# A batch loop of 16 equal steps: one key and one value tile each, maxima one step behind, context split by quarters

## The reference

```python
# 1. cross attention, 16 heads of 32
qh = layernorm(x) @ wq + bq;  kh = ctx @ wk + bk;  vh = ctx @ wv + bv     # keys: 2048 per batch
x  = x + softmax(qh kh^T / sqrt(32)) vh @ wo + bo
# 2. causal linear attention with relu features, then an MLP 512 -> 2048 -> 512 with GELU
# 3. gated feed-forward 512 -> 1408 -> 512 with blockwise FP4 rounding of activations and weights
```

## Time and profile before

| | |
|---|---|
| median of 3 runs | 3425.43 us (3423.25 to 3429.36) |
| profiled execution | 3425.2 us, span 3423.4 us |
| granted TensorE clock, mean | 0.998 of full |
| PE busy | 3384.3 us (99%) |
| PE weight loads busy | 2628.8 us (77%) |
| DVE busy | 2221.6 us (65%) |
| POOL busy | 2081.4 us (61%) |
| ACT busy | 1200.4 us (35%) |

### The profile page before, as it was taken

One profiled execution on the slowest core, in us unless ns is written; L12 is line 12 of the kernel. 1 busy time (PEld: TensorE's weight loads), 2 busy tenths in 40 slices (PEclk: granted clock), 3 DMA queues, 4 the chain that ended last, 5 costly groups with the idle time before them and its releaser, 6 DMA issues.

```text
span 3423.4 us, 77272 instructions
## 1 busy us (share of the span) xinstructions
PE 3384.3 (99%) x31304; PEld 2628.8 (77%) x31304; DVE 2221.6 (65%) x3425; ACT 1200.4 (35%) x1655; POOL 2081.4 (61%) x1210
## 2 busy tenths in 40 slices
PE   8999999999999999999999999999999999999999
PEld 6777777777777777777777777777777788878887
DVE  6556556555655655655565565566776688789997
ACT  2244343443434434344344343444223322321111
POOL 3277877878777887778877878762545400023332
PEclk9999999999999999999999999999999999999999
DMA  4111110111101100101011010122222333410000
GB/s 152 50 44 38 38 38 29 47 38 38 38 30 47 50 29 35 50 27 51 29 44 42 26 51 29 48 75 76 72 87 83 128 102 101 130 65 19 25 18 19
DMA packets 83368, 182.96 MB, mean 53 GB/s; under 512 B 7184, under 2 KB 43152, under 8 KB 73872
## 3 DMA queue, kind: packets, MB, share of 16 engines
q1 hardware_dynamic: 83088, 178.63, 15.1%
HBM read 140.59 MB, written 38.01 MB: 52 GB/s over the span
## 4 chain that ended last, share of the span: by engine, by line
PE 92%; DVE 4%; issue 2%; ACT 1%; POOL 1%; DVEq 0%; ACTq 0%; POOLq 0%
PE a_bank L100 67%; PE a_bank L1408 8%; PE a_bank L1453 7%; PE a_bank L1417 6%; DVE x_probsT L1263 1%; PE a_bank L712 1%; PE a_bank L2421 1%; ACT x_probsT L1152 0%; PE a_bank L723 0%; PE a_bank L1472 0%; PE a_bank L1441 0%; PE a_bank L777 0%; PE a_bank L781 0%; DVE s_rden L653 0%; PE a_bank L1426 0%
## 5 line engine op out<-in xcount | busy, mean ns | idle before, releaser
L1251 DVE TENSOR_REDUCE x_maxima<-a_bank 128x1 f32<-128x512 f32 x960 | 608.5, 683 | 741.0 <-PE a_bank L1408 741.0
L949 POOL TENSOR_TENSOR x_pairs<-x_probsT 128x1024 f32<-128x1024 f32 x240 | 571.7, 2382 | 298.2 <-ACT x_probsT L1152 292.9
L100 PE MATMUL a_bank<-x_wv,x_ctx 128*128 128x512 f32 x3072 | 746.0, 396 | 1.1 <-ACT q_out L224 1.1
L100 PE MATMUL a_bank<-x_ctx,x_wk 128*128 128x512 f32 x3072 | 743.3, 396 | 0.0
L1152 ACT ACTIVATE x_probsT<-x_probsT 128x1024 f32<-128x1024 f32 x480 | 507.8, 1058 | 642.1 <-DVE x_probsT L1263 642.1
L100 PEld LDWEIGHTS a_bank<-x_wv,x_ctx 128*128 128x128 f32 x3072 | 563.7, 188 | 167.2 <-DVE x_maxima L1251 27.3
L100 PEld LDWEIGHTS a_bank<-x_ctx,x_wk 128*128 128x128 f32 x3072 | 564.7, 188 | 136.7 <-issue 11.9
L1263 DVE TENSOR_TENSOR x_probsT<-a_bank,x_shift_all 128x1024 f32<-128x1024 f32 x480 | 578.7, 1216 | 138.2 <-ACT x_shift_all L1169 120.1
L1417 PEld LDWEIGHTS a_bank<-x_q,x_k 32*128 32x128 f32 x7680 | 240.8, 186 | 115.5 <-issue 63.0
L1147 ACT ACTIVATE x_v<-a_bank 128x512 f32<-128x512 f32 x256 | 153.1, 598 | 420.6 <-PE a_bank L100 420.6
L1077 POOL TENSOR_TENSOR x_ctx<-x_ctx_raw,x_ctx 128x2048 fp32r<-128x2048 f32 x64 | 293.1, 4579 | 5.0
(11 more groups left out here) (207 smaller groups left out, 3992.8 us busy)
## 6 DMA issues: line engine op xcount, KB each, us to landing
x_ctx_raw<-in_ctx SPq DMA_DIRECT2D x64, 1024.0 KB, 4.8
m_ff_src<-in_w_ff SPq DMA_DIRECT2D x44, 192.0 KB, 2.5
wq_ff<-m_ff_dst SPq DMA_DIRECT2D x44, 192.0 KB, 1.8
attT<-x_out_halves SPq DMA_DIRECT2D x16, 512.0 KB, 2.8
s_attT<-attT SPq DMA_DIRECT2D x16, 512.0 KB, 4.0
m_w_raw<-in_w SPq DMA_DIRECT2D x32, 256.0 KB, 2.9
f_w_in<-wq_ff SPq DMA_DIRECT2D x22, 256.0 KB, 3.5
q_x<-in_x SPq DMA_DIRECT2D x16, 256.0 KB, 4.3
```

Source lines behind the costliest of these rows:

```text
L100: mm = pe.matmul(out, lhs[a], rhs[b], start=first and n == 0, stop=last and n == 2)
L949: eng.tensor_tensor(pairs[:], probs(i, s)[:, :, 0:2], probs(i, s)[:, :, 2:4], ALU.add).then_inc(paired, 1)
L1251: dve.tensor_reduce(maxima[:, c, g * HG + j:g * HG + j + 1], banks[:, j], AX.X, ALU.max).then_inc(maxed, 1)
```

## The change

- The batch loop's body is `back(i)` (steps 8 to 15) and then `front(i + 1, i)` (steps 0 to 7 of the next batch), for 14 turns. `front(0)` stands ahead of it, `back(14)` behind it.
- Every step s does `top(s - 1)`, `score(s)`, in even steps two `weigh`, then one key item (`key_bank`: bank 5 in even steps, 4 in odd ones) and one value item (`value_bank`: bank 4 in step 0, bank 0 in all others). The value item of step s is tile s - 4 modulo 16: tiles 12 to 15 of a batch are made in its own steps 0 to 3. `top(15)` and the last two `weigh`, into bank 1, stand behind step 15.
- `score(0)` waits for the last `gather` of the batch before. Step 1 waits for the value item of step 0 to be copied out; then come `denominators` of the batch before, into bank 3, and `top(0)`.
- Two spreads stand between the key and the value item of step 0, one in step 1, one in step 2.
- The context is loaded and split in tiles of 128 rows (`load_tile`, `split_tile`): 256 KB, and two GpSimd operations on 128x512 elements in each step. A tile's split waits for the value item of the same step, whose buffer it overwrites. The key item of steps 0, 4, 8 and 12 waits for all the tiles before it.
- GpSimd's four operations that end a batch are spread over the steps 3 to 6 of the next. The division is done in two halves, in steps 1 and 2, in place. The last gathers write the sums to `x_sums_out`, so that `x_acc` is not read by GpSimd. Each result goes out in two transfers.
- In the first batch the tiles 12 and 13 leave the code ahead of the loop; after the loop four value tiles are made and not two, and the denominators of batch 14 come behind them.

```diff
-            def macro(i):                                    # tensor
...
+            def keys(i, s):
+                c, t = divmod(s, DC)
+                if t == 0:
+                    pe.wait_ge(ctx_made, START + tiles_made(i, s))
+                pe.wait_ge(maxed, START + HG * (NS - 1) + i * (HG * NS) + (HG * s + key_bank(s) - HG + 1))
+                item(i + 1, "k", c, t, key_bank(s), (lambda: turn(i)) if s == 0 else None)
+
+            def values(i, s):
+                if s:
+                    pe.wait_ge(shifted, START + i * (2 * NS) + (2 * s + 1))
+                item(i, "v", *value_tile(s), value_bank(s))
+
+            def step(i, s, past=None):
+                if s == 0:
+                    pe.wait_ge(gathered, START + i * TWINS)
+                    pe.wait_ge(shifted, START + i * (2 * NS))
+                    pe.wait_ge(v_ready, START + values_done(i, -1))
+                    score(i, 0)
+                else:
+                    if s == 1:
+                        pe.wait_ge(v_ready, START + values_done(i, 0))
+                        pe.wait_ge(shift_kept, START + shift_at(i, HG + 2))
+                    if s in (2, 3):
+                        pe.wait_ge(shift_kept, START + shift_at(i, HG + s + 1))
+                    if past is not None and s == 1:
+                        pe.wait_ge(shifted, START + i * (2 * NS) + 2)
+                        denominators(past, 3)
+                    pe.wait_ge(gathered, START + i * TWINS + (s - 1) // 2)
+                    top(i, s - 1)
+                    if past is not None and s == 1:
+                        pe.wait_ge(den_out, START + (past + 1))
+                    pe.wait_ge(shifted, START + i * (2 * NS) + 2 * s)
+                    pe.wait_ge(v_ready, START + values_done(i, s - 1))
                     score(i, s)
+                if s and s % 2 == 0:
+                    await_maxed(i + 1, s - 1, 1)
+                    weigh(i, s - 2)
+                    weigh(i, s - 1)
+                keys(i, s)
+                if s < 3:
+                    for g in ((0, 1), (2,), (3,))[s]:
+                        spread(i, g)
+                values(i, s)
...
+                top(i, NS - 1)                                # back(i), behind step 15
                 pe.wait_ge(shifted, START + i * (2 * NS) + 2 * NS)
+                weigh(i, NS - 2, b=1)
+                weigh(i, NS - 1, b=1)
...
+            def split_tile(i, s):                             # gpsimd
+                hi, lo = (a[:, (s // TPC + 1) % 2, :, cols(s % TPC, P)] for a in ctx_t)
+                raw_t = tile_raw[s % 2]
+                pool.wait_ge(ctx_loaded[s % 2], START + (WHOLE * 16 * (1 - s % 2)) + i * (8 * NS) + 16 * (s // 2 + 1))
+                pool.wait_ge(v_done, START + values_done(i, s))
+                pool.tensor_tensor(hi, raw_t[:], one[:].to_broadcast([P, DC, P]), ALU.mult).then_inc(ctx_made, 1)
+                pool.wait_ge(ctx_made, START + tiles_made(i, s) + 1)
+                pool.tensor_tensor(lo, raw_t[:], hi.bitcast(F32), ALU.subtract).then_inc(ctx_made, 1)
...
+            def step(i, s, past=None, ahead=True):
+                if ahead or s < NS - TPC:
+                    split_tile(i, s)
+                add_up(pool, i, s)
+                if past is not None and 3 <= s < 7:
+                    (normalise, add_bias, out_hi, out_lo)[s - 3](past)
...
+            def first_step(i, past):                          # scalar
                 place_rows(i)
                 copy_spread(i, 0)
+                keys(i, 0)
+                copy_spread(i, 1)
+                exp(i, 0, 0)
+                values(i, 0)
+                if past is not None:
+                    copy_den(past)
+                exp(i, 0, 1)
...
+            def step(i, s, past=None):                        # vector
+                if s:
+                    maximum_by_head(i + 1, s - 1, tops, (0, 1))
+                add_shift(i, s, 0)
+                if s:
+                    maximum_by_head(i + 1, s - 1, tops, (2, 3))
+                add_shift(i, s, 1)
+                if s and s % 2 == 0:
+                    gather(i, s // 2 - 1)
+                if past is not None and s in (1, 2):
+                    invert(past, s - 1)
...
+                maximum_by_head(i + 1, NS - 1, tops, (0, 1, 2))   # back(i), behind step 15
                 gather(i, TWINS - 1)
+                maximum_by_head(i + 1, NS - 1, tops, (3,))
                 negate(i + 1)
...
+            for v in range(TPC):                              # tensor, behind the loop
+                await_maxed(LAST, NS - 1, (2, HG)[v > 0])
+                if v >= 2:
+                    await_item(LAST, "v", NKC - 1, v - 2)
+                item(LAST, "v", NKC - 1, v, (5, 7)[v % 2], (lambda: turn(LAST)) if v == 0 else None)
+            await_item(LAST, "v", NKC - 1, TPC - 2)
+            denominators(LAST - 1, 5)
```

More of the change, by code:

```diff
@@ L858, in attention_phase, with key_bank, value_bank, value_tile @@
     LAST = B - 1
[L859 to L873, removed]
+    ALONE = 8
+    WHOLE = NKC + 1
+    SET_UP = 4
+    KEYS_PER = 1
+    def key_bank(s):
+        return 4 + (s + 1) % 2
+    def value_bank(s):
+        return 0 if s else 4
+    def value_tile(s):
+        return divmod((s - DC) % NS, TPC)
     with ExitStack() as stack:
@@ L1091, in add_bias @@
                 pool.wait_ge(out_made, START + i * 3 + 2)
[L1092 to L1111, removed]
+                pool.tensor_tensor(lo[:], sums_out[:], hi[:].bitcast(F32), ALU.subtract).then_inc(out_made, 1)
@@ new lines, in finish, with front @@
+            def finish(i, first=True):
+                if first:
+                    normalise(i)
+                for part in (add_bias, out_hi, out_lo):
+                    part(i)
+            def step(i, s, past=None, ahead=True):
[4 more added lines that the diff above has]
+                    (normalise, add_bias, out_hi, out_lo)[s - 3](past)
+            def front(i, past=None):
+                for s in range(ALONE):
+                    step(i, s, past)
@@ L1113, in _, with back @@
+            def back(i, ahead=True):
+                for s in range(ALONE, NS):
+                    step(i, s, ahead=ahead)
             sc.raise_start(pool, SIGNALLED_BY["gpsimd"])
@@ L1128, in _ @@
             q.await_stored(pool, B // MT - 1)
-            with looped(nc, pool, 0, B - 2) as i:
-                macro(i)
-            macro(B - 2, ahead=False)
+            front(0)
+            with looped(nc, pool, 0, LAST - 1) as i:
+                back(i)
+                front(i + 1, i)
+            back(LAST - 1, ahead=False)
+            pool.wait_ge(k_done, START + B * NS)
+            late.split_output_weights(pool, one)
+            finish(LAST - 1)
             late.pool_step(pool, FIRST, lambda: pool.wait_ge(scored, START + LAST * NS + (NS - DC + 1)))
-            late.gpsimd(pool, lambda: add_bias(LAST))
+            late.gpsimd(pool, lambda: finish(LAST, first=False))
             late.after.gpsimd(pool)
@@ L1198, in _, with front, back @@
+            def front(i, past=None):
+                first_step(i, past)
+                for s in range(1, ALONE):
+                    step(i, s)
+            def back(i):
+                for s in range(ALONE, NS):
+                    step(i, s)
             sc.raise_start(act, SIGNALLED_BY["scalar"])
@@ L1443, in last_score, with weigh @@
                 mm.then_inc(scored, 1)
[L1445 removed]
+            def weigh(i, s, last=False, b=HG):
                 c, g = divmod(s, DC)
```

396 lines of the change are left out of this document (190 added, 206 removed).

## The result

The changed kernel takes 3445.23 us (median of 4 runs, 3444.65 to 3446.83) against 3425.27 before: ratio 1.0062, 95% interval 1.005 to 1.0074. It is slower by 0.6%. The forecast was 3446, in a range of 3431 to 3462. The span of the profiled execution grew from 3423.4 to 3442.9, 19.5 us.

What follows compares the result with a forecast made beforehand. TensorE, busy 99%, was taken as the bound. Over 14 turns 10 us for the longer batch and 7 for GpSimd's lateness, plus 1.5 and 2 once, make 20.5 on 3425.2: 3446 us, range 3431 to 3462.

Steps and rivals of the forecast that it cites:

- The bound: Whole kernel: TensorE, busy 99% of the span, sets the time; only fewer gaps and switches there can gain.
- The steps: TensorE from step 1 to step 15 of a batch: 8.0 + 9.9 + 110.8 us, a spread between items costing 0.36.
- First stall: Head of a batch: TensorE waits before score(0) for VectorE's last gather, 0.7 us.
- Second stall: Step 1: TensorE waits before the denominators until ScalarE has copied step 0's value item from bank 4, 0.8 us.
- Third stall: Step 8's key item waits for GpSimd's split of step 7: 0.5 us a batch, 14 x 0.5 = 7 us.
- the rival to which I gave 0.22: GpSimd is in time at step 8, by quicker signals or shorter operations, so no wait there: 3439 us; chance 0.22.
- The rival in which the quarters cost more than contiguous operations: GpSimd falls behind at step 8: strided quarters cost more, or a load slips; 14 x 1.4 = 20 us, 3466; chance 0.12.
- the even order saves this 0.8: Batch without the two head stalls: 140.2 us against 140.96, as fewer items stand alone on TensorE.
- Once: Outside the turns: batch 0's wait before the denominators and the wait at turn behind the loop, together 1.5 us.
- The input sum: Behind the loop: normalise starts 5.6 us later, TensorE waits 1.4 for the sum; 2 us taken, between 0 and 4.
- Loads: Context in 16 loads of 256 KB instead of four of 1 MB: landing in 5.2 us, worth nothing either way.

Runs made afterwards that it cites:

- the added operations: Changed kernel plus one or two unused 128x512 GpSimd operations a batch in step 6: 3455.97 and 3469.27 us, beside 3423.91 for the kernel before.
- the one variant nearly without waits: Changed kernel with denominators before the value-tile wait, half a value tile before score 0, transposition right behind it, spreads mid key item, spread copies earlier: 3426.06 us.

## Why the prediction was right

- **The bound.** TensorE sets the time, and the change is worth what it does to TensorE's gaps: shown by all variants.
- **The steps.** From top(0) to top(15) I had 8.0 + 9.9 + 110.8 = 128.7; it is 128.6, with 7.89 (1317.65 - 1309.76) and 9.83 for the steps with a spread. A spread between two items costs 0.26, not 0.36.
- **First stall.** Right in place and cause, mis-sized: 1.0 for 0.7. The weighs start 1.07 after the top, the gather waits for them and not for the third maximum, and from the gather's end at 1299.90 to the score 0.34 passes; I had allowed less than 0.1, and left out the register operations of the waits.
- **Second stall.** 0.95 for 0.8, for the same reason: the copy ends at 1308.45, the denominators start 0.31 later.
- **Third stall.** Wrong: forecast 0.5, measured 0, the rival to which I gave 0.22. The step that failed is the length of a job. I put a gap of 0.08 behind each operation; the trace has it only between operations that hand on a result. Independent ones follow with none (1370.66 after 1369.44 + 1.27). A job is 7.45 (1361.99 to 1369.44) and not 7.61, which is 0.5 over three jobs; the three operations that end a batch are 0.35 shorter in sum, mostly for the same reason, and the wait of 0.25 ahead of the split of step 6, which I didn't have, takes most of that back. From the start of step 5 the split of step 7 ends after 28.4 (1373.07 - 1344.63), where I had 29.0; the key item comes up after 28.75, as forecast. The mechanism itself is real, as the added operations show. The rival in which the quarters cost more than contiguous operations is out: the splits take 1.04 and 1.27.
- **What it makes.** 13.8 + 13.3 us of waits in the 14 heads, and 16.0 us of time: 14 x 1.14 against the forecast 14 x 1.2. That number is good by luck, because two errors cancel: the head is forecast 0.6 too short (12.9 for 13.53), and 0.5 is for a stall that isn't there. Without its waits a batch would be 142.1 - 1.9 = 140.2, against 140.96. That the even order saves this 0.8 is argued and not shown: the one variant nearly without waits has 140.8, or 140.4 with its last waits, 0.4 on average, taken off.
- **Once.** 1.5 forecast and 1.5 measured, but not by its parts: the second stall of batch 0 is 0.69 and the wait ahead of the transposition behind the loop 0.28, and where the rest comes from is open. The input sum is 2 and 2.0, with a PE wait of 1.44 where I had 1.4. Only the 1.5 that show at the fourth score are sure: from the first score to the end, the eight traces that have the same code there take 1132.3 to 1135.1.
- **Loads.** A tile lands in 3.0 us, where the earlier trace rows had 5.2, and no engine in the loop waited for one, so the size of the loads changed nothing.

Open is why the lower clock follows every second of the waits of 2.2 us, and whether the variant with the denominators moved behind the loop is really faster. Untried is the order of the waits: with the one that ends last put last, the 0.34 and 0.31 should come down to 0.05, by an estimate from these rows 14 x 0.54 = 8 us.

## What to carry to other kernels

A loop body that is even in its steady part can still lose at its seam. Ask what the first instruction of the bottleneck engine in the new turn waits for, and which independent work could stand ahead of that wait: here the denominators, moved ahead of one wait, gave 12 of 21 us. Put the wait that ends last behind the others, if their values have to be worked out anew in each turn (an estimate of 8 us here, not tested). Where the waits belong to one chain, filling the early one with more work than it has room for delays the chain; start the chain earlier first. And an engine with 38% idle time may have no slack at the one deadline that counts: add an operation and see.

## What the runs showed of the hardware that I had not expected

- How soon a TensorE that stands still resumes goes with the waits that stand behind the one that ends last. Over the ten traces it starts 0.05 to 0.06 us after the end of the instruction that releases it with none behind (175 cases), 0.13 to 0.15 with one or two (162 of 164), 0.31 to 0.34 with three (140). The register operations of the waits are in the trace, 0.1 us apart; a variant with nothing but their order changed was not run.
- A wait of 2.2 us in an otherwise full TensorE was followed by the lower granted clock behind every second such wait, and not behind the others of the same length; price 1.65 us each. A wait of 2.0 us in batch 0 was followed by it in one variant and not in another. With waits of 1.0 and 1.6 at that place, and of 1.7 to 1.8 ahead of the key item of step 8, no head showed it.
- GpSimd's operations have 0.08 us between them if the second waits for what the first wrote, and none otherwise: then the second starts 0.05 before the recorded end of the first.
